# Cross-attention rows regrouped: 14 tiles of 128 (head, token) rows per batch instead of 16 heads of 112 rows

## The reference

```
x = x + tanh(g_xattn) * xattn(layernorm(x), ctx)        # x (32, 112, 256), ctx (32, 375, 128)
x = x + tanh(g_ffn) * ffn(layernorm(x))                 # 14 routed experts (top 2) and 2 shared ones
xattn(q, kv): 16 heads of 64
    scores = (q Wq)(kv Wk)^T / 8;  softmax over the 375 context rows
    out = concat_heads(softmax @ (kv Wv)) Wo + bo
ffn(h): each expert silu(rmsnorm(h) W1) W2, 256 -> 512 -> 256
```

## Time and profile before

| | us |
|---|---|
| median of 3 runs | 1568.28 (1566.87 to 1570.26) |
| the profiled execution, its own time | 1573.0 |
| its span, first to last instruction | 1571.0 |
| of it up to the end of the attention | 1108.6 |

### The profile page before, as it was taken

The page is one execution under the profiler, slowest core; times in us unless marked ns, Lnnn a source line. Parts: engine busy times, 40 slices in busy tenths (PEclk is TensorE's granted clock), DMA queues, the critical chain, the costliest instruction groups (busy, mean ns, idle before and its releaser), DMA issues. The chain is left out here.

```text
span 1571.0 us, 34457 instructions
## 1 busy us (share of the span) xinstructions
PE 1501.7 (96%) x10158; PEld 1390.8 (89%) x10158; DVE 1154.0 (73%) x2884; ACT 1011.7 (64%) x2641; POOL 418.4 (27%) x662
## 2 busy tenths in 40 slices
PE   6999999999999999999999999999599989999998
PEld 6899999999999999899999999998389978778887
DVE  5888878888788888888888888887587534344448
ACT  5777777777777777777777777776343334444452
POOL 1012413134041331403224131310100125555530
PEclk9999999999999999999999999999899999999999
DMA  4010311202212022121212112010512335653234
GB/s 116 6 48 16 105 70 51 100 14 100 75 45 100 20 100 76 45 74 45 100 39 82 68 51 100 14 66 7 185 69 108 121 133 203 225 175 128 77 132 198
DMA packets 55295, 136.95 MB, mean 87 GB/s; under 512 B 10480, under 2 KB 38144, under 8 KB 51648
## 3 DMA queue, kind: packets, MB, share of 16 engines
q1 hardware_dynamic: 48608, 118.01, 21.6%
q0 software_dynamic: 6624, 18.13, 3.7%
HBM read 86.69 MB, written 49.43 MB: 87 GB/s over the span
## 5 line engine op out<-in xcount | busy, mean ns | idle before, releaser
L616 ACT ACTIVATE prob<-bank,nmax 112x375 f32<-112x375 f32 x512 | 295.8, 578 | 242.3 <-DVE nmax L705 240.8
L688 DVE TENSOR_TENSOR pT_lo<-bank,pT_hi 125x336 fp32r<-125x336 f32 x512 | 256.7, 501 | 94.2 <-ACT pT_hi L628 91.9
L705 DVE TENSOR_REDUCE nmax<-bank 112x1 f32<-112x375 f32 x512 | 276.1, 540 | 32.7 <-PE bank L484 27.2
L538 PE MATMUL bank<-keep_ident,prob 112*125 112x112 f32 x1536 | 253.8, 274 | 15.5 <-DVE pT_lo L688 15.4
L538 PEld LDWEIGHTS bank<-keep_ident,prob 112*125 112x125 f32 x1536 | 225.4, 188 | 46.5 <-issue 32.8
L628 ACT CAST pT_hi<-bank 125x336 fp32r<-125x336 f32 x512 | 223.1, 436 | 1.3 <-PE bank L538 1.2
L482 PE MATMUL bank<-attend_wvo_hi,zT_hi 128*112 128x256 f32 x512 | 179.3, 350 | 0.6 <-DVE zT_lo L688 0.6
L482 PE MATMUL bank<-attend_kvT_hi,qp_hi 128*112 128x376 f32 x512 | 171.4, 335 | 0.8 <-ACT prob L616 0.7
L484 PE MATMUL bank<-attend_kvT_lo,qp_hi 128*112 128x376 f32 x512 | 171.0, 334 | 0.0
L483 PE MATMUL bank<-attend_kvT_hi,qp_lo 128*112 128x376 f32 x512 | 170.7, 333 | 0.0
L621 ACT ACTIVATE prob<-prob,prob_inv 112x375 f32<-112x375 f32 x256 | 153.2, 598 | 1.6 <-DVE prob_inv L711 0.4
(11 more groups left out here) (245 smaller groups left out, 3811.5 us busy)
## 6 DMA issues: line engine op xcount, KB each, us to landing
w_split<-we_split SPq DMA_DIRECT2D x14, 2048.0 KB, 6.8
keep_weights<-w_split SPq DMA_DIRECT2D x14, 2048.0 KB
we_in<-in_w SPq DMA_DIRECT2D x28, 512.0 KB, 5.7
over_y_all<-y_rows SPq DMA_DIRECT2D x14, 512.0 KB, 8.9
kv_in<-in_ctx SPq DMA_DIRECT2D x32, 187.5 KB
h_rows<-hrow SPq DMA_DIRECT2D x32, 112.4 KB, 2.2
over_h_in<-h_rows SPq DMA_DIRECT2D x7, 514.0 KB, 6.6
x_in<-in_x SPq DMA_DIRECT2D x16, 224.0 KB, 2.7
```

The costliest lines, as they stand in the source:

```text
L538: last = nc.tensor.transpose(T[s % 2][0:MP, c * N:(c + 1) * N], prob[:, s % NB, c * MP:(c + 1) * MP], ident[0:N, 0:N])
L616: nc.scalar.activation(prob[:, s % NB, :], S[s % 3][0:N, 0:M], ACT.Exp, bias=nmax[:, s % NB:s % NB + 1], accum_out=psum_[:, s % NB:s % NB ...
L688: return nc.vector.tensor_tensor(dst, src, hi.bitcast(F32), ALU.subtract)
L705: nc.vector.tensor_reduce(nmax[:, s % NB:s % NB + 1], S[s % 3][0:N, 0:M], AX, ALU.max, negate=True).then_inc(max_ready, 1)
```

## The change

A batch's 16 x 112 = 1792 (head, token) rows are cut into 14 tiles of 128, and a pair has 28 steps. Scores, maximum, exponential, normalisation and turn work on tiles of 128 rows; query products, sums and projections stay with heads and quads of heads (448 rows, 3.5 tiles). `qp` is laid out by batch and then by (head, token), so that a tile is 128 neighbouring columns. `pT` becomes a ring of seven tiles (two quads). A quad's sums start five steps behind its last tile, now behind the turn in the step for the first third, and its projections nine steps behind; where two quads overlap, a step has two projections. `JOBS` and the norms have new steps. The ring `prob` has 7 places instead of 8, and step 27 uses scores bank 1. On GpSimd the split of an expert stands behind the second context split and the first `ln2_root`.

```
-        NB = 8
+        NB = 7
-        qp = {q: buf("qp_" + q, [P, H, 2 * N], F32R) for q in ("hi", "lo")}
+        qp = {q: buf("qp_" + q, [P, 2, H * N], F32R) for q in ("hi", "lo")}
-        prob = buf("prob", [N, NB, M])
-        pT = {q: buf("pT_" + q, [MP, 2, MC, 4 * N], F32R) for q in ("hi", "lo")}
+        prob = buf("prob", [P, NB, M])
+        pT = {q: buf("pT_" + q, [MP, MC, 2 * QUAD], F32R) for q in ("hi", "lo")}
-        JOBS = [(3, "q", 4), (7, "q", 5), (9, "q", 6), (11, "q", 7), (13, "kv", 1), (16, "xT", 0), (19, "q", 0),
-                (23, "q", 1), (27, "q", 2), (29, "kv", 0), (31, "q", 3)]
+        JOBS = [(2, "q", 4), (4, "q", 5), (6, "q", 6), (8, "q", 7), (11, "kv", 1), (14, "xT", 0), (17, "q", 0),
+                (19, "q", 1), (22, "q", 2), (24, "kv", 0), (26, "q", 3)]
+        def last_tile(qd):
+            return (QUAD * (qd + 1) - 1) // P
+        def quads_at(p, s, after, first):
+            for qd in range(8):
+                at = last_tile(qd) + after
+                if at == s:
+                    yield p, qd
+                if at - STEPS == s and not first:
+                    yield p - 1, qd
+        def score_bank(s):
+            return S[1 if s == STEPS - 1 else s % 3]
+        def ring_place(s):
+            return slice(s % 7 * P, (s % 7 + 1) * P)
                 for phase, after in (("add", 0), ("aggr", 1), ("roots", 3), ("apply", 6)):
-                    t = H * b + 29 + after
+                    t = STEPS // 2 * b + 26 + after
...
                 if XT in jobs:
                     ln_root(p + 1)
-                if XT in jobs and not first:
-                    split_expert(p - 1)
                 split_context(p, 1)
                 if not first:
                     ln2_root(2 * p - 1)
+                if XT in jobs and not first:
+                    split_expert(p - 1)
                 add_bias(p, 1)
...
-                need(pe, exp_done, g - 1 if s < 2 else g - 2)
-                three(S[s % 3][0:N, 0:MW], [qp[q][:, h, b * N:(b + 1) * N] for q in ("hi", "lo")],
+                need(pe, exp_done, g - 1 if s in (1, STEPS - 1) else g - 2)
+                rows = slice(j * P, (j + 1) * P)
+                three(score_bank(s)[:, 0:MW], [qp[q][:, b, rows] for q in ("hi", "lo")],
...
+            def behind(p, s, jobs, first):
+                for c in (1, 2):
+                    for quad in quads_at(p, s, 5 + c, first):
+                        sums(*quad, c)
+                for k in jobs:
+                    if JOBS[k][0] == s:
+                        side(p, k)
+                if s - 3 < STEPS and (tile := back(p, s - 3, first)):
+                    turn(*tile)
+                for quad in quads_at(p, s, 5, first):
+                    sums(*quad, 0)
+                for j in range(4):
+                    for quad in quads_at(p, s, 9 + j, first):
+                        project(*quad, j)
...
-                need(act, z_done, 8 * p + s // 4 - 1)
+                need(act, z_done, 8 * p + (P * (s - 6) - 1) // QUAD + 1)
...
-                    if s % 4 == MC and (quad := back(p, s // 4 - 2, 8, first)):
+                    for quad in quads_at(p, s, 7, first):
                         ctx_sums(*quad)
...
-                    if XT in jobs and s == 4:
+                    if XT in jobs and s == 3:
                         ln_stats(p + 1)
-                    if XT in jobs and s == 5:
+                    if XT in jobs and s == 4:
                         ln_aggregate(p + 1)
-                    if XT in jobs and s == 10:
+                    if XT in jobs and s == 9:
                         ln_apply(p + 1)
```

More of the change, by code:

```diff
@@ L269, in side_bank, with heads_of, back, units_of @@
             return banks[k - OWN] if isinstance(p, int) and p < 0 else SIDE
+        def heads_of(part, u):
+            return qp[part][:].rearrange("p b (h n) -> p h b n", n=N)[:, 2 * u:2 * u + 2]
         def kv_job(p, b):
             return job_index(p, KV1) if b else job_index(p - 1, KV0)
[L275 to L279, removed]
+        def back(p, s, first):
+            if s >= 0:
+                return p, s
+            return None if first else (p - 1, s + STEPS)
+        def last_tile(qd):
[9 more added lines that the diff above has]
+            return S[1 if s == STEPS - 1 else s % 3]
+        def units_of(t):
+            return [u for u in range(8) if 2 * u * N // P == t]
+        def ring_place(s):
+            return slice(s % 7 * P, (s % 7 + 1) * P)
         LN_P, LN2_P = 5, 7
@@ L545, in sums @@
                 if c == 0:
-                    pe.wait_ge(pT_lo, 2 * H * p + 4 * qd + 4)
+                    pe.wait_ge(pT_lo, STEPS * p + last_tile(qd) + 1)
                     if qd % 4 == 0:
@@ L572, in body @@
                 first = isinstance(p, int) and p == 0
[L573 to L583, removed]
-            body_over_pairs(pe, body)
[L585 to L591, removed]
+                for s in range(STEPS):
+                    scores(p, s)
+                    behind(p, s, jobs, first)
+            body_over_pairs(pe, body)
+            for s in range(STEPS, last_tile(7) + 13):
+                behind(PAIRS - 1, s, (), True)
         def steps(p, s):
-            return 2 * H * p + s
+            return STEPS * p + s
         @block.scalar
@@ L655, in body @@
                 nc.scalar.preload_act_table_set("natural_log_exp_and_others")
-                for s in range(2 * H):
-                    if head := back(p, s - 4, 2 * H, first):
-                        turned(*head)
+                for s in range(STEPS):
+                    if tile := back(p, s - 4, first):
+                        turned(*tile)
                     exps(p, s)
-                    if s % 2 == 0 and (head := back(p, s - 1, 2 * H, first)):
-                        norm(*head)
-                    if s % 4 == MC and (quad := back(p, s // 4 - 2, 8, first)):
+                    if s % 2 == 0 and (tile := back(p, s - 1, first)):
+                        norm(*tile)
+                    for quad in quads_at(p, s, 7, first):
                         ctx_sums(*quad)
@@ L666, in body @@
                             side(p, k)
-                    if s == 7 and XT in jobs:
+                    if s == 6 and XT in jobs:
                         ln_roots(p + 1)
@@ L673, in _ @@
             last = PAIRS - 1
-            turned(last, 2 * H - 4)
-            norm(last, 2 * H - 1)
+            turned(last, STEPS - 4)
+            norm(last, STEPS - 1)
             for s in (3, 2, 1):
-                turned(last, 2 * H - s)
+                turned(last, STEPS - s)
             ctx_sums(last, 6)
@@ L784, in body @@
                     maxima(p, s)
[L785 to L789, removed]
+                    if tile := back(p, s - 4, first):
+                        turned(*tile)
+                    if tile := back(p, s - 1, first):
+                        norm(*tile)
+                    for quad in quads_at(p, s, 7, first):
                         ctx_sums(*quad)
```

63 lines of the change are left out of this document (32 added, 31 removed).

## The result

The kernel after takes 1587.4 us (median of 4 runs, 1583.9 to 1589.3), the kernel before 1567.6: a ratio of 1.012 (95% interval 1.010 to 1.015). It is slower by about 20 us, where I had forecast 33 us faster, and 1587 lies outside the range of 1508 to 1560. The profiled execution of after took 1583.9 us, the lowest of its four, and that of before, 1573.0 us, lies above all four of its other executions, so the traces show only 11 of the 20 us; they do not show where the rest lies. The stage behind the attention takes what it took, within about 1 us.

The account below looks back on a forecast made before the run. TensorE was taken as the bound, VectorE close behind; 61.3 work + 2.6 Z waits + 0.4 rest = 64.3 against 66.6 us a pair, 33 us in all, so 1535 us, range 1508 to 1560.

Parts of the forecast that it names:

- part 1: TensorE, 28 steps instead of 32 a pair: scores and turns save 3.0 us, leaving 61.3 us of work a pair.
- the load of 128 columns is not covered: Rival, scores products on TensorE: 13 ns more each gives back 1.1 us a pair, 1551 us; chance 0.04.
- a turn costs in proportion to its rows: Rival, turns on TensorE: 0.37 us each gives back 1.1 us a pair, 1551 us; chance 0.06.
- The other engines: ScalarE and VectorE: VectorE's busy time falls from 55.8 to about 52 us a pair, worth nothing by itself.
- Part 4: New order, single bank Z: TensorE waits 1.7 and 0.9 us at two short gaps, 2.6 us a pair, from 0 to 5.
- the two other short gaps: Z gaps at steps 17 to 18 and 3 to 4: a query job covers them, 3.3 against 2.3 us.
- for the rest I leave 0.4 us: Remaining TensorE waits a pair: output bank at step 12, turns near steps 16 and 21, together 0.4 us.
- Part 3: GpSimd's expert split moved to steps 16 to 22, where query jobs give VectorE slack; up to 1.8 us of waits gone.
- 1.8 of the 2.3 us of waits as gone: The old TensorE waits a pair, ahead of pT_lo: moving GpSimd's split removes up to 1.8 of 2.3 us.
- slower: Rival, zT_lo waits at all four short gaps, 6.8 us; decides from 5.3 us a pair; 1590 us; chance 0.06.
- The tail: End of the attention: one step less but the same chain of copies, so nothing gained.

Follow-up runs that it names:

- the repaired kernel before: Kernel before (32 steps) with ScalarE's table load behind the copy of step 0 and GpSimd's long subtractions in four: 1567.8 us, ratio 1.000.
- four small edits: Kernel after with Z's copy ahead of the normalisation, query job at step 27, table load behind the first copy, subtractions in four: 1533.1 us, 0.978 of before.

## Why the prediction was wrong

**The work: right.** Scores product, turn and projection cost what part 1 took (0.17 us apart, 0.69 against 0.68 for turn and projection), and a pair's own work is 61.6 us against the 61.3 of the forecast, so it fell by 2.9 us and not by 3.0. The rivals in which the load of 128 columns is not covered, or a turn costs in proportion to its rows, are out. With the first goes the rule that part 1 took for it from the Trainium skill, "TensorE: Matmul & The Clock Gate", Part 3 (The mechanism): here the products lie 173.5 ns apart with loads of 189 ns each, and lay 171.3 ns apart with loads of 174 ns before, so of the longer load only 2 ns a product show, 0.2 us a pair.

**The other engines: right in size.** VectorE is busy 52.3 us a pair (said: 52). That it "is worth nothing by itself" was right as well, and was the hint that I left: an engine that is 84% busy before and 78% after has little room, and in the short steps 1 and 21 it came too late.

**Part 4, the waits for Z: right in place, a little too high.** I said 1.7 and 0.9 us at steps 11 and 25, with the two other short gaps covered; the trace has 1.27 and 0.90, and the other two gaps have no wait. That the normalisation lengthens the chain is shown, its 0.6 us roughly: with the copy first, the two steps lost 0.41 and 0.69 us. That the `xn` operations add 0.8 us in front is shown only in part: without them there, step 11 fell by 0.64, but the time came back at once.

**The step that failed is "for the rest I leave 0.4 us".** It measured 3.4 us: 1.61 at step 1, 0.94 at step 21, 0.37 at 15, 0.31 at 8, 0.19 at 22. Three judgements stand behind it. The waits at 15 and 8 I did not trace.

- *Step 1.* I never laid ScalarE's table load into the order. In before the whole wait at step 1 is 0.18 us, and I had summed ScalarE's busy time without asking what stood beside it. Both cures of this wait work singly (0.75 us a pair for the query job, 0.74 for the load's place) and together leave 0.16 us of the 1.61. So about half of the wait was the load, and about half the three steps in a row without a job.
- *Step 21.* Part 3 said that the query jobs at 17, 19 and 22 give VectorE slack for the moved split. The mean does, but one normalisation was shut out for 2.2 us just ahead of the two steps 20 and 21 that have no job. Cutting the GpSimd operation removed the 0.94 us.
- *Part 3, "1.8 of the 2.3 us of waits as gone".* In the kernel before, the move alone costs 20 us. And the repaired kernel before shows that the wait at step 18 stays when the collisions are cut short. The share of before's waits that I put down to the collisions was argued from nearness in time. The 0.5 us that this step left standing of the old waits went into no term of the sum but the 0.4.

In sum: 61.3 + 3.0 forecast, 61.6 + 5.6 measured: 0.3 us more work, 0.4 less at `Z`, 3.0 more in the rest. (The sum also takes 33 us for 15.5 pairs at 2.3, which would be 36; that changes nothing here.) The point of decision that I gave for "slower", 5.3 us of waits, was about right, but the mechanism that I gave it was not: the waits were at two of the four gaps of `Z` and not at all four, and more of them stood elsewhere. The tail, which I took at nothing, is 1 us longer: from the last scores to the last projection 13.5 us before and 14.5 after, on the same chain of copies.

Was the gain there? Yes: with four small edits that touch none of the 28 steps' work, the kernel reaches 1533.1 us. That this is near the 1535 of the forecast is chance, since the forecast was for another kernel: its 63.7 us a pair are 61.6 of work and 2.1 of waits, against 61.3 and 3.0.

## What to carry to other kernels

When an order written out by hand is made shorter, write down for every step how long the bounding engine takes, and look for runs of two or three short steps: there the chain of copies behind them is on the path, whatever the mean busy share says. Lay every occasional operation of the other engines (a table load, a norm, a long operation of GpSimd) into that list, one by one; a single remainder term is no place for them. And judge a moved operation by what it stands beside in the new order: the same move cost one kernel 20 us and spared the other 13.

## What the runs showed of the hardware

VectorE's normalisation was shut out for up to 2626 ns beside GpSimd operations of 2.4 us, and up to 1530 ns beside ones of 1.3 us: cutting the long operation of an engine that nobody waits for was worth 16 us. A loop body without the one line that names a common function set had 94 table loads of 1283 ns instead of 16, and cost 78 us. Loads of 128 stationary columns, 189 ns each, stayed covered behind products of 376 moving columns that start 173.5 ns apart.
